# A 512-wide graph layer: 16 gathered tiles a block with a loop for the rest, and its loads moved to another queue

## The reference

```
agg = segment_sum(h[src], dst)
h   = relu(((1 + eps) * h + agg) @ w + b)
```

## Time and profile before

| | us |
|---|---|
| median of 3 runs | 4946.31 |
| lowest, highest | 4939.7, 4948.61 |
| the profiled execution, its own time | 4950.88 |
| its span | 4949.2 |
| the 512-wide layer, in the trace | about 3120 to 4345 |

### The profile page before, as it was taken

One profiled execution on the slowest core, in us unless ns is written; L12 is line 12 of the kernel. 1 busy time (PEld: TensorE's weight loads), 2 busy tenths in 40 slices (PEclk: granted clock), 3 DMA queues, 4 the chain that ended last, 5 costly groups with the idle time before them and its releaser, 6 DMA issues. The chain is left out here.

```text
span 4949.2 us, 70593 instructions
## 1 busy us (share of the span) xinstructions
PE 3788.6 (77%) x15851; PEld 2474.8 (50%) x15852; DVE 2212.0 (45%) x7809; ACT 1419.7 (29%) x2721; POOL 2665.5 (54%) x4165
## 2 busy tenths in 40 slices
PE   3886645555555555885899999688888888879999
PEld 1233334444444444775677777344444444467777
DVE  6996756666666666345111121222222223222222
ACT  3982222222222222235344444100000010033333
POOL 6780066666666665013544444366666666655554
PEclk9999967777777777985999999899999999899999
DMA  4442133333333333026767666477777676656665
GB/s 137 174 190 68 55 93 90 88 92 92 93 89 93 93 93 81 0 59 176 200 186 203 190 183 180 148 207 212 207 210 209 206 213 204 183 167 188 200 183 170
DMA packets 347068, 730.73 MB, mean 148 GB/s; under 512 B 77999, under 2 KB 171821, under 8 KB 342577
## 3 DMA queue, kind: packets, MB, share of 16 engines
q0 software_dynamic: 176144, 461.72, 33.3%
q10 hardware_dynamic: 100802, 157.63, 10.2%
q1 hardware_dynamic: 69980, 109.80, 6.5%
HBM read 622.28 MB, written 106.64 MB: 147 GB/s over the span
## 5 line engine op out<-in xcount | busy, mean ns | idle before, releaser
L901 POOL DMA_INDIRECT a_gathered<-table,record x850 | 807.2, 950 | 688.0 <-issue 368.3
L2265 POOL DMA_INDIRECT l_gathered<-table,record x782 | 760.5, 972 | 478.2 <-issue 275.5
L2455 PE MATMUL bank<-l_gathered,l_onehot 128*125 128x512 f32 x1564 | 774.8, 649 | 189.5 <-DMA l_gathered<-table,record 108.0
L1829 POOL DMA_INDIRECT l_gathered<-table,record x578 | 546.6, 946 | 487.8 <-PE bank L2037 218.4
L1250 PE MATMUL bank<-a_gathered,a_onehot 128*125 128x264 f32 x1700 | 564.4, 490 | 101.0 <-DVE a_gathered L1054 85.6
L2455 PEld LDWEIGHTS bank<-l_gathered,l_onehot 128*125 128x125 f32 x1564 | 312.5, 205 | 629.8 <-issue 464.7
L1943 ACT ACTIVATE l_part<-l_packed 128x1000 fp32r<-128x1000 bf16 (+1 forms) x396 | 411.6, 1070 | 578.6 <-DMA l_packed<-adjacency 176.6
L1250 PEld LDWEIGHTS bank<-a_gathered,a_onehot 128*125 128x125 f32 x1700 | 389.3, 241 | 201.9 <-issue 67.5
L2018 PE MATMUL bank<-rows_last,l_part 125*125 125x512 f32 x1650 | 407.4, 404 | 35.1 <-ACT l_part L1943 22.4
L2018 PE MATMUL bank<-rows_first,l_part 125*125 125x512 f32 x1650 | 407.3, 406 | 35.1 <-ACT l_part L1943 35.1
L2018 PEld LDWEIGHTS bank<-rows_first,l_part 125*125 125x125 f32 x1650 | 309.0, 188 | 127.1 <-issue 44.6
(11 more groups left out here) (282 smaller groups left out, 5613.4 us busy)
## 6 DMA issues: line engine op xcount, KB each, us to landing
l_packed<-adjacency ACTq DMA_DIRECT2D x264, 250.0 KB
adjacency<-d_stage SPq DMA_DIRECT2D x33, 1562.5 KB
l_packed<-adjacency ACTq DMA_DIRECT2D x132, 281.2 KB
l_gathered<-table,record POOLq DMA_INDIRECT x1360
a_gathered<-table,record POOLq DMA_INDIRECT x850
table<-rows_first POOLq DMA_DIRECT2D x50, 250.0 KB, 3.4
table<-l_work ACTq DMA_DIRECT2D x50, 250.0 KB
l_source_rows<-table ACTq DMA_DIRECT2D x50, 250.0 KB
```

The source lines that it names most:

```text
L901: pool.indirect_dma_start(out=gathered0[s][:, j * TW:(j + 1) * TW], out_offset=None, in_=table0, in_offset=bass.IndirectOffsetOnAxis(ap=re ...
L1829: pool.indirect_dma_start(out=gathered[g][:, j, :], out_offset=None, in_=table, in_offset=bass.IndirectOffsetOnAxis(ap=record[k.t][:, j, 0 ...
L2265: pool.indirect_dma_start(out=gathered[:, j * w:(j + 1) * w], out_offset=None, in_=table, in_offset=bass.IndirectOffsetOnAxis(ap=record[t] ...
L2455: last = pe.matmul(total[0:NB, 0:w], onehot[t][:, j, :], rows[:, j, :], start=False, stop=(j == T - 1), skip_group_check=True)
```

## The change

The layer gets its own tile count WT = 16 (RW = 2048 edges), and QUARTERS of 4 tiles each. The first 16 tiles are written out without a loop, so their waits compare with constants or with the register of the step loop, and the counters go. A block's further edges, from the smaller of first_edge[b] + 2048 and first_edge[b + 1] to first_edge[b + 1], go to a loop Fori(lo, hi, 128). The lower bounds stand in a table, rest_from, that DVE makes with three operations when the layer starts. The same loop serves the tabled blocks, with dense_ends as before.

In that loop POOL itself loads the 128 records, waits for them and gathers 128 rows (gather_rest). DVE makes the one-hot matrix (onehot_rest, the last stage of its step), PE multiplies ahead of the closing matmul L2463. The matmul with zeros that opened a block's sum (L2448) is gone; the first tile starts it.

SP runs nothing in this layer. ACT issues the own rows of block b and the record of block b + 1 at the head of step b, ahead of copy_turned; the records of blocks 0 and 1 come before the first packed loads.

The core of the diff:

```
+WT = 16
+RW = WT * P
...
-                QUARTERS = [(0, 4), (4, 8), (8, 12), (12, T)]
+                QUARTERS = [(0, 4), (4, 8), (8, 12), (12, WT)]
...
-                def edge_range(engine, s, i):
+                def rest_range(engine, s, i):
 
                     b = block_at(s, i)
                     if tabled(s, i):
                         ends = [dense_ends[0:1, e, bass.ds(b, 1)] for e in range(2)]
                     else:
-                        ends = [first_edge[0:1, bass.ds(b + e, 1)] for e in range(2)]
+                        ends = [rest_from[0:1, bass.ds(b, 1)], first_edge[0:1, bass.ds(b + 1, 1)]]
                     lo, hi = [engine.value_load(end, min_val=0, max_val=E) for end in ends]
                     return lo, hi
...
-                    def load_few(lo, hi):
-                        with sp.Fori(lo, hi, OV) as at:
-                            sp.wait_ge(few_used, few_of(sp, few) + 1)
-                            sp.dma_start(few_record[:, :], edges[bass.ds(at, OV), :]).then_inc(few_loaded, 16)
-                            sp.reg_add(few, few, 1)
-
-                    def load_block(s, i):
-                        lo, hi = edge_range(sp, s, i)
-                        if tabled(s, i):
-                            load_few(lo, hi)
-                        else:
-                            t = record_of(s, i)
-                            with sp.Fori(lo, hi, RE) as at:
-
-                                sp.wait_ge(round_gathered[t], count_of(sp, rounds[t]) + 1)
-                                sp.dma_start(record[t][:, :, :].rearrange("p j c -> p (j c)"),
-                                             edges[bass.ds(at, RE), :].rearrange("(p j) c -> p (j c)", j=T)).then_inc(record_loaded[t], 16)
-                                sp.reg_add(rounds[t], rounds[t], 1)
-                        sp.wait_ge(own_used[s], i + 1)
-                        sp.dma_start(own[s][:, :], block_rows(table, block_at(s, i))).then_inc(own_loaded[s], 16)
-
-                    over_steps(sp, [(load_block, 0)])
...
-                    def gather_few(lo, hi):
-                        with pool.Fori(lo, hi, OV) as at:
+                    def gather_rest():
+                        lo, hi = [pool.snap(reg, min_val=0, max_val=E) for reg in bounds]
+                        with pool.Fori(lo, hi, P) as at:
                             before = few_of(pool, few)
+                            wait_apart(pool, few_used, before + 1, 1)
+                            pool.dma_start(few_record[:, :], edges[bass.ds(at, P), :]).then_inc(few_loaded, 16)
                             wait_apart(pool, few_loaded, before * 16 + 16, 16)
                             pool.indirect_dma_start(
                                 out=few_rows[:, :], out_offset=None, in_=table,
@@ -2249,35 +2231,32 @@
                             pool.reg_add(few, few, 1)
 
                     def gather(s, i):
-                        lo, hi = [pool.snap(reg, min_val=0, max_val=E) for reg in bounds]
                         if tabled(s, i):
-                            gather_few(lo, hi)
+                            gather_rest()
                             keep(load_next(s, i))
                             return
                         t = record_of(s, i)
-                        with pool.Fori(lo, hi, RE) as at:
-                            wait_apart(pool, record_loaded[t], count_of(pool, rounds[t]) * 16 + 16, 16)
-                            before = count_of(pool, filled)
-                            for q, (j0, j1) in enumerate(QUARTERS):
-
-                                wait_apart(pool, quarters_used, before * NQ + q + 1, 1)
-                                for j in range(j0, j1):
-                                    pool.indirect_dma_start(
-                                        out=gathered[:, j * w:(j + 1) * w], out_offset=None, in_=table,
-                                        in_offset=bass.IndirectOffsetOnAxis(ap=record[t][:, j, 0:1], axis=0),
-                                    ).then_inc(rows_gathered[q], 16)
-                                    if j == QUARTERS[2][1]:
-                                        found = load_next(s, i)
-                            pool.reg_add(rounds[t], rounds[t], 1)
-                            pool.reg_add(filled, filled, 1)
+                        found = None
+                        wait_apart(pool, record_loaded[t], round_of(s, i) * 16 + 16, 16)
+                        for q, (j0, j1) in enumerate(QUARTERS):
+
+                            wait_apart(pool, quarters_used, filled_of(s, i) * NQ + q + 1, 1)
+                            for j in range(j0, j1):
+                                pool.indirect_dma_start(
+                                    out=gathered[:, j * w:(j + 1) * w], out_offset=None, in_=table,
+                                    in_offset=bass.IndirectOffsetOnAxis(ap=record[t][:, j, 0:1], axis=0),
+                                ).then_inc(rows_gathered[q], 16)
+                                if j == QUARTERS[2][1]:
+                                    found = load_next(s, i)
+                        gather_rest()
                         keep(found)
 
-                    keep(edge_range(pool, 0, 0))
+                    pool.wait_ge(rest_ready, 1)
+                    keep(rest_range(pool, 0, 0))
                     over_steps(pool, [(gather, 0)])
...
+                    dve.tensor_copy(first_f[:, :], first_edge[:, :]).then_inc(rest_steps, 1)
+                    dve.wait_ge(rest_steps, 1)
+                    dve.scalar_tensor_tensor(rest_f[:, :], first_f[:, 0:BLOCKS], float(RW), first_f[:, 1:BLOCKS + 1],
+                                             ALU.add, ALU.min).then_inc(rest_steps, 1)
+                    dve.wait_ge(rest_steps, 2)
+                    dve.tensor_copy(rest_from[:, :], rest_f[:, :]).then_inc(rest_ready, 1)
+                    dve.wait_ge(rest_ready, 1)
...
+                    def onehot_rest(s, i):
+                        lo, hi = rest_range(dve, s, i)
+                        with dve.Fori(lo, hi, P) as at:
                             before = few_of(dve, few)
                             dve.wait_ge(few_loaded, before * 16 + 16)
                             dve.wait_ge(few_used, before + 1)
                             dve.tensor_scalar(few_relative[:, :], few_record[:, 1:2].bitcast(F32),
-                                              minus_base[0:OV, bass.ds(block_at(s, i), 1)], None, ALU.add).then_inc(few_placed, 1)
+                                              minus_base[:, bass.ds(block_at(s, i), 1)], None, ALU.add).then_inc(few_placed, 1)
                             dve.wait_ge(few_placed, before + 1)
-                            dve.tensor_scalar(few_onehot[:, :], column[0:OV, 0:NB], few_relative[:, :], None,
+                            dve.tensor_scalar(few_onehot[:, :], column[:, 0:NB], few_relative[:, :], None,
                                               ALU.is_equal).then_inc(few_ready, 1)
                             dve.reg_add(few, few, 1)
...
-                    over_steps(dve, [(rounds_of, 0), (finish, 1), (halve, 4)], split_source, 6, AHEAD + 1)
+                    over_steps(dve, [(onehots, 0), (finish, 1), (halve, 4), (onehot_rest, 0)], split_source, 6, AHEAD + 1)
...
+                    def load_records(s, i):
+                        if tabled(s, i):
+                            return
+                        t, r = record_of(s, i), round_of(s, i)
+                        lo = act.value_load(first_edge[0:1, bass.ds(block_at(s, i), 1)], min_val=0, max_val=E)
+                        act.wait_ge(round_gathered[t], r + 1)
+                        act.dma_start(record[t][:, 0:WT, :].rearrange("p j c -> p (j c)"),
+                                         edges[bass.ds(lo, RW), :].rearrange("(p j) c -> p (j c)", j=WT)).then_inc(record_loaded[t], 16)
+
+                    def load_own(s, i):
+                        act.wait_ge(own_used[s], i + 1)
+                        act.dma_start(own[s][:, :], block_rows(table, block_at(s, i))).then_inc(own_loaded[s], 16)
...
+                    over_steps(act, [(load_weights, 0), (load_own, 0), (load_records, -1), (copy_turned, 1), (store, 2), (keep_upper, 5)], cast_source, AHEAD, AHEAD + 1)
...
+                    def sums(s, i):
                         rows = gathered.rearrange("p (j c) -> p j c", c=w)
                         total = total_of(s, i)
...
+                        if not tabled(s, i):
                             t = record_of(s, i)
                             pe.wait_ge(sums_read[s], i + 1)
-
-                            pe.matmul(total[0:NB, 0:w], zeros[:, 0:NB], zeros[:, 0:w], start=True, stop=True)
-                            with pe.Fori(lo, hi, RE) as at:
-                                pe.wait_ge(onehot_ready[t], count_of(pe, rounds[t]) + 1)
-                                before = count_of(pe, emptied)
```

(71 more changed lines are left out.)

58 lines of the change are left out of this document (23 added, 35 removed).

## The result

The changed kernel takes 5067.39 us (median of 4 runs, 5053.4 to 5074.18), the kernel before beside it 4943.01. The ratio is 1.0243, 95% interval 1.020 to 1.0286: slower by 124 us. The forecast was 5048, range 4925 to 5190. Its profiled execution has a span of 5071.3 us, 122 more than the earlier trace rows.

The account below looks back on a forecast made before the run. POOL's gathers with the pause behind each block were taken to bound the 512-wide layer. 4950.88 + 90 (44 blocks) + 12 (tabled blocks) = 5053, less 4.6 for the profiled run: 5048 us; 8-in-10 range 4925 to 5190.

Parts of the forecast that it names:

- The sign: Whole kernel: slower at 0.72, same at 0.10, faster at 0.18.
- the steady distance: Between POOL's block starts in the 512-wide layer: 27.3 us against 25.24, +2.05 a block, paid by 44 blocks.
- The loop runs once on an empty range: Further-round loop: equal bounds still run its body once, so all 50 blocks do a further round and no gather is saved.
- Rival C: The further-round loop is skipped for 40 blocks: 38 us less, 4908 us; chance 0.14.
- The wait for the further record: POOL's stream before the further gather: 3.2 us from record issue to landing plus 0.7 to POOL's start.
- The pause behind it: POOL after the further gather, before the next block: 2.4 us, ends 1.43 and 4.24.
- rival B: The further record's wait falls into POOL's present pause of about 4 us: 4935 to 4960, say 4946 us; chance 0.14.
- Tabled blocks: Their further rounds in POOL's stream grow from 1.25 to 4.85 us for three of them: 12 us (0 to 16).
- Loads from ACT: Record and own loads moved to ACT land some 3 us later, with 7 us of cover: no cost.
- rival D: ACT becomes late and records come after POOL wants them: 2 us beyond cover a block adds 88, 5136 us; chance 0.10.
- PE and DVE: Their added waits for the further record or rows in each block: 3 us of cover on PE, idle stretches on DVE; no cost.

Follow-up runs that it names:

- e_skip_sp: The changed kernel with the further-round loops behind a branch taken only where hi > lo, and both loads on SP: 4905.61 us, ratio 0.9913.
- e_skip: The changed kernel with each further-round loop (POOL, DVE, PE) behind a branch taken only where hi > lo, loads still on ACT: 5002.38 us, ratio 1.0108.
- e_sp: The changed kernel with the loads of records and own rows back on SP, all further rounds still running: 4995.58 us, ratio 1.0098.
- e_early: The changed kernel with SP loading the further round's record ahead, ACT keeping the other loads, all further rounds running: 5046.42 us, ratio 1.0212.
- third group: Runs on a third chip, kernel before 4932.43 us: the changed kernel 1.0259, with the branch 1.0122, with branch and loads on SP 0.9936.
- e_skip_parts: The changed kernel with the branch around empty further rounds and packed loads on SP, records and own rows on ACT; second chip: 4841.44 us, ratio 1.0345.
- e_17_skip_sp: The changed kernel with WT = 17, further rounds behind a branch never taken, loads on SP; second chip: 4684.19 us, ratio 1.0007.
- e_skip_sp2: e_skip_sp once more on the third chip, against the kernel before there: 4899.49 us, ratio 0.9936.

## Why the prediction was right, and where its working was not

The sign, the time and the steady distance (27.35 measured, 27.3 forecast) came out. The working behind them is half right, and that the sum agrees is luck: its terms were off in both directions. Measured for a steady block: 19.9 for the 16 gathers, 5.5 for the further record, 1.0 for its gather, 0.9 to the next block.

- *The loop runs once on an empty range.* Right: 50 further gathers, 6 with the branch. It was read from counts in other layers, and it decided the sign. Rival C needed the loop to be skipped; e_skip_sp is C made true, at 0.9913 and 0.9936. C's own number, 4908, was near it (4905.61), though there the loads are on SP; with ACT's loads C's kernel is e_skip, slower than before.
- *The wait for the further record.* Sized as 3.2 us from issue to landing and 0.7 to POOL's start, 3.9. In the steady blocks of the changed kernel it is 0.59 of issue and 4.92 of idle, 5.5; in e_sp 0.59 and 3.93, 4.5. The rows of POOL's own transfers came from a stretch in which no gathers were under way. The fixed 2.0 us of the Trainium skill (DMA: Bandwidth & Descriptors, Anatomy of one DMA — SWDGE (gpsimd) path), named beside it, were further off there: with the 0.7 to POOL's start they make 2.7, and the shortest idle in a steady block is 2.87 with 0.59 of issue ahead of it. In three of the four tabled blocks of the changed kernel they fit, 2.04 to 2.09 of idle behind 0.56 of issue; in e_sp only in the last one, and the other three take 4.3 to 4.8. The last of the layer in the changed kernel:

```profile
4439.10 0.97 POOL L2227 DMA_INDIRECT l_few_rows<-table,l_few_record  x1 [2.04 <-DMA l_few_record<-edge_records]
```
- *The pause behind it.* Sized as 2.4, with ends 1.43 and 4.24. Measured 0.94 in the changed kernel and 0.34 in e_sp. The pause is not paid on top: it is gone where POOL has waited for the further record, and back in blocks of e_early, where POOL does not wait for it. This is rival B's mechanism, to which I gave 0.14, and it holds: with the loads on SP a steady block costs 0.54 us more than before, not 2.05. My argument against B, that the pause moves with POOL's last gather, was true and did not tell against it.
- *Tabled blocks.* 12 us forecast, 28 measured in e_sp (133.2 − 105.3), 35 in the changed kernel. I priced the record's wait and left out the one before it, on the single buffer that PE has to give back (4.33 us).
- *Loads from ACT.* This is the step that failed: the term was put at nothing, with 7 us of cover, and rival D at 0.10. They cost 1.45% with the further rounds (1.0243 to 1.0098) and 1.9% without (1.0108 to 0.9913; third group 1.0122 to 0.9936), 72 to 97 us. The record is late in two ways. One is the landing, for which I took 3 us: on the second chip it is 11.8 and 12.5 us from ACT, and e_skip_parts shows the record late without packed issues. The other is the date of the issue, and here rival D was right in kind. In all seven steady blocks of the changed kernel in which POOL stands for the record, the load is issued 24.1 to 25.2 us after the previous block's start, and POOL goes on 4.3 to 5.3 us after the issue, so the landing was quick. One of them, issue and POOL:

```profile
3789.63 7.70 ACTq L2367 DMA_DIRECT2D l_packed<-adjacency  x3
3797.39 0.29 ACTq L2400 DMA_DIRECT2D l_own<-table  x1
3798.74 0.34 ACTq L2395 DMA_DIRECT2D record<-edge_records  x1
...
3803.57 0.96 POOL L2245 DMA_INDIRECT l_gathered<-table,record  x1 [4.14 <-DMA record<-edge_records]
```

These seven waits are only 23 of the 72 us, a quarter of rival D's 88; the longer wait for the further record is 38 more (0.99 in 38 blocks). Why that record lands later beside ACT's loads was not tried.
- *PE and DVE.* No cost, right so far as the traces go: in the changed kernel POOL's idle "<-PE bank" is 25.2 us, most of it ahead of the second and third block (9.8 and 8.3).

So of the 2.4%: the 17th tile saved gives −0.9% (e_skip_sp), the empty rounds and their record waits +1.85% on top (e_sp), ACT's loads +1.45% (the changed kernel). Taken in the other order the same two costs are 1.35% and 1.95%, so they are not independent. I had the total right by luck: with e_sp's rows the pause was too high by 2.06 us a block, 91 us in all, against 72 for ACT's loads, 27 for the further record's wait and 16 for the tabled blocks that were missing. The range was wide enough for either.

**What stays open.** What the pause is. The trace of the kernel before has it, 3.83 us in the mean of the steady blocks, and so have e_skip_sp on the first chip and e_skip_sp2 on the third. On the second chip 714 gathers follow one another in e_17_skip_sp without one; its time and that of the kernel before are the same there. The trace says "remote" or "PE bank" by turns. What it does show is POOL's own queue running empty. From the end of the last gather at 3682.23 to POOL's next start at 3686.34 in the kernel before, q0 moves 201 packets, and in the last 1.24 us of that stretch two:

```profile
q0 software_dynamic: 201, 0.64, 46.1%
...
q0 software_dynamic: 2, 0.00, 0.9%
```

In the last microsecond before POOL starts a block, q0 moves 2 or 3 row packets in the median of the steady blocks; in e_17_skip_sp it moves 48. So the pause lasts about as long as the gathered rows need to land. Whether POOL waits for that is not shown, but it would explain why the pause passes inside the wait for the further record. Whether the record would still be late behind ACT's source rows and store alone, with the own rows on SP, was not tried. Nor was a second buffer for the further round.

## What to carry to other kernels

A small load that an engine waits for should not be issued on a queue that carries large ones, even when its issue comes early enough: compare its landing on each queue as well as the date of its issue. A loop over a range from memory may run its body once on an empty range; count it in the trace, and put a branch around it if the body has a wait. And when two unknown terms make up a sum, name the run that takes each away before trusting that the sum agrees.

## What the runs showed of the hardware that I had not expected

- The same kernel is 4948 and 4932 us on two chips and 4679 on a third. The whole layer is different there: over 600 us of steady work POOL is busy 456 us at 244 GB/s (e_17_skip_sp), in the kernel before, in the earlier trace rows, 661 of 1010 at 208 GB/s.
- The move of the loads costs more on the faster chip: 4.0% there with 17 tiles, 1.9% on the others with 16. With the loads on ACT the blocks are about as far apart on both (25.3 and 25.9 to 26.0 us); with them on SP they are 21.6 and 24.0 to 24.1. I take it that the pause covered part of the record's landing; no run shows that alone.

```profile
3300.00:3900.00 600.00, 542.71 (x1536) 271.89 (x1535) 194.91 (x672) 67.32 (x140) 455.88 (x474) 0.99 0.81 244
```

This row is the window of e_17_skip_sp: length, busy PE, PEld, DVE, ACT, POOL, granted clock, DMA share, GB/s.
